# Reciprocals of the softmax sums broadcast as two f16 halves, with new instruction lists, in a four-batch transformer layer

## The reference

```
x = x + attn(layernorm(x)) ; x = x + ffn(layernorm(x))
attn: qkv = x @ Wqkv ; 16 heads of 32 ; a = softmax(mask(q k^T / sqrt(32))) ; (a @ v) @ Wo
ffn:  g = silu(x @ w1q^T) * (x @ w3q^T) ; g @ w2q^T      (w1, w3: 1365 x 512, w2: 512 x 1365)
ternary: s = mean|w| ; q = clip(round(w / s), -1, 1) * s
```

## Time and profile before

| | |
|---|---|
| three timed runs | 578.77, 579.03, 580.35 us (median 579.03) |
| the profiled execution | 580.78 us, of which the profile's span is 579.0 |
| TensorE busy | 508.0 us |
| VectorE, GpSimd, ScalarE busy | 411.8, 368.4, 330.2 us |
| mean granted TensorE clock | 0.941 of 2.4 GHz |

### The profile page before, as it was taken

One profiled execution on the slowest core, in us unless ns is written; L12 is line 12 of the kernel. 1 busy time (PEld: TensorE's weight loads), 2 busy tenths in 40 slices (PEclk: granted clock), 3 DMA queues, 4 the chain that ended last, 5 costly groups with the idle time before them and its releaser, 6 DMA issues.

```text
span 579.0 us, 11497 instructions
## 1 busy us (share of the span) xinstructions
PE 508.0 (88%) x4092; PEld 237.9 (41%) x4092; DVE 411.8 (71%) x1026; ACT 330.2 (57%) x833; POOL 368.4 (64%) x460
## 2 busy tenths in 40 slices
PE   2669754857999999999999999999999998839997
PEld 2224322333445444544444444454444454314443
DVE  6599787697899877966888879578878771523421
ACT  4769866777756875645467875363666752012320
POOL 3077689777968976776667887556668782312320
PEclk9689955878999999999999999999999999869999
DMA  8939978999889756387596565675783548030001
GB/s 312 316 30 278 193 170 160 252 200 211 153 141 162 145 124 131 56 158 194 108 167 143 90 131 97 141 180 114 101 173 75 109 87 208 9 63 1 0 37 72
DMA packets 224205, 79.52 MB, mean 137 GB/s; under 512 B 213226, under 2 KB 213226, under 8 KB 224148
## 3 DMA queue, kind: packets, MB, share of 16 engines
q1 hardware_dynamic: 224148, 78.79, 65.0%
HBM read 20.97 MB, written 4.19 MB: 43 GB/s over the span
## 4 chain that ended last, share of the span: by engine, by line
PE 69%; POOL 9%; DMA 8%; SPq 5%; DVE 4%; issue 2%; ACT 2%; DVEq 0%; ACTq 0%
PE work L1120 46%; PE work L1280 13%; DMA early<-early 4%; PE work L1239 4%; PE score_bank L1197 4%; POOL early L654 4%; PE work L1210 2%; DMA rows<-in_L_attn_x 2%; POOL late L687 2%; POOL early L687 1%; SPq L517 1%; DVE early L986 1%; DMA w_ternary<-early 1%; POOL rows L669 1%; DMA late<-rows 1%
## 5 line engine op out<-in xcount | busy, mean ns | idle before, releaser
L654 POOL TENSOR_TENSOR early<-early 128x512 f16<-128x512 f32 (+1 forms) x192 | 193.7, 1021 | 40.4 <-DVE early L986 26.5
L762 ACT ACTIVATE early<-early,exp_bias 128x512 f32<-128x512 f32 (+3 forms) x256 | 140.8, 551 | 76.7 <-POOL exp_bias L661 76.5
L1120 PE MATMUL work<-late,w_ternary 128*128 128x512 f16 (+1 forms) x704 | 158.9, 384 | 10.3 <-DMA late<-rows 10.3
L974 DVE CUSTOM_DVE_ANT_0 early<-score_bank,mask,scalars 128x512 f32<-128x512 f32 (+3 forms) x256 | 131.7, 543 | 32.7 <-POOL early L654 20.4
L986 DVE CAST early<-early 128x512 f16<-128x512 f32 (+1 forms) x148 | 99.5, 690 | 18.1 <-ACT early L762 14.7
L1120 PEld LDWEIGHTS work<-late,w_ternary 128*128 128x128 f16 (+1 forms) x704 | 69.2, 101 | 93.9 <-issue 17.9
L1120 PE MATMUL work<-xt,wqkv_hi 128*128 128x512 f16 x256 | 80.7, 398 | 2.9 <-DVE wqkv_lo L936 2.0
L1280 PE MATMUL work<-w_ternary,late 128*128 128x512 f16 (+1 forms) x352 | 77.7, 379 | 0.0
L679 POOL TENSOR_TENSOR late<-late 128x512 f16<-128x512 f32 (+1 forms) x44 | 51.3, 1168 | 40.1 <-ACT late L799 39.4
L792 ACT ACTIVATE late<-work,scalars 128x512 f32<-128x512 f32 (+1 forms) x44 | 30.0, 682 | 53.0 <-DVE late L1027 36.1
L1120 PE MATMUL work<-xt,wqkv_lo 128*128 128x512 f16 x128 | 51.0, 398 | 0.0
(11 more groups left out here) (103 smaller groups left out, 702.4 us busy)
## 6 DMA issues: line engine op xcount, KB each, us to landing
rows<-in_L_attn_x SPq DMA_DIRECT2D x16, 256.0 KB, 3.0
x_res<-in_L_attn_x SPq DMA_DIRECT2D x12, 256.0 KB, 3.2
out_y<-x_res SPq DMA_DIRECT2D x12, 256.0 KB, 2.8
late<-in_L_ffn_w SPq DMA_DIRECT2D x4, 682.5 KB, 5.5
early<-in_L_ffn_w SPq DMA_DIRECT2D x3, 768.0 KB, 12.8
late<-in_L_ffn_w SPq DMA_DIRECT2D x3, 768.0 KB, 6.7
late<-in_L_attn_Wqkv SPq DMA_DIRECT2D x4, 512.0 KB, 7.2
late<-in_L_attn_Wqkv SPq DMA_DIRECT2D x1, 1024.0 KB, 9.8
```

The costliest lines, as they stand in the source:

```text
L654: pool.tensor_tensor(split_view(s, p, 1, h), raw_view(s, p, h), split_view(s, p, 0, h), ALU.subtract).then_inc(low_done, 1)
L762: last = act.activation(piece, piece, ACT.Exp, bias=bias, accum_out=sums[:, s % 2, at:at + 1])
L974: last = dve.tensor_tensor_reduce(raws[n % RAWS][:, off:off + cols], score_bank[h][:, off:off + cols], mask[:, S - cols:S], scalar(exp_sca ...
L1120: last = pe.matmul(bank, lhs, rhs, start=(n == 0), stop=(n == len(terms) - 1))
```

## The change

The reciprocals are scaled by 2^24 and split in two f16 halves. The broadcast then takes two f16 products per head and row tile in place of one f32 product, accumulated in the same bank, and the copy out of the bank divides by 2^24. All five lists are replaced by new ones. SyncE's waits ahead of the transposes of x name the last readers per bank.

```diff
@@ constants and tiles
+INVERSE_UNIT = 2.0 ** 24
+        ident_half = sb("ident_half", [P, P], F16)
+        inverse_hi = sb("inverse_hi", [P, 2, ST * HG], F16)
+        inverse_lo = sb("inverse_lo", [P, 2, ST * HG], F16)
@@ SyncE, turn_rows
-                    for used in [(m, GROUPS * b - 1) for m in "qk"] + [("v", b - 1, j) for j in range(ST)]:
-                        full(sp, used)
+                    readers = [(m, GROUPS * (b - 1) + g) for m in "qk" for g in range(GROUPS)]
+                    readers += [("v", b - 1, j) for j in range(ST)]
+                    for n_bank in range(NW):
+                        full(sp, max((r for r in readers if bank_of(r) == n_bank), key=turn_of))
@@ GpSimd, constants
+                pool.wait_ge(ident_made, 1)
+                pool.tensor_copy(ident_half[:], ident[:]).then_inc(ident_turned, 1)
@@ ScalarE, inverse_copy
-                act.activation(o_sb[:], work[bank_of(step)][:], ACT.Copy).then_inc(work_free[bank_of(step)], 1)
+                act.activation(o_sb[:], work[bank_of(step)][:], ACT.Copy, scale=1 / INVERSE_UNIT).then_inc(work_free[bank_of(step)], 1)
@@ VectorE, invert
-                dve.reciprocal(inverse[:, s % 2, :], sums[:, s % 2, :]).then_inc(inverted, 1)
+                dve.reciprocal(inverse[:, s % 2, :], sums[:, s % 2, :]).then_inc(reversed_sums, 1)
+                dve.wait_ge(reversed_sums, s + 1)
+                dve.tensor_scalar(inverse_hi[:, s % 2, :], inverse[:, s % 2, :], INVERSE_UNIT, None,
+                                  ALU.mult).then_inc(inverse_hi_done, 1)
+                dve.wait_ge(inverse_hi_done, s + 1)
+                dve.scalar_tensor_tensor(inverse_lo[:, s % 2, :], inverse[:, s % 2, :], INVERSE_UNIT, inverse_hi[:, s % 2, :],
+                                         ALU.mult, ALU.subtract).then_inc(inverted, 1)
@@ TensorE, inverse_rows
+                if s == 0:
+                    pe.wait_ge(ident_turned, 1)
                 for u in range(ST):
-                    for h in range(HG):
-                        of_head = inverse[:, s % 2, u * HG + h:u * HG + h + 1].to_broadcast([P, HD])
-                        last = pe.matmul(work[bank][HD * h:HD * (h + 1), u * P:(u + 1) * P], of_head, ident[:],
-                                         start=True, stop=True, skip_group_check=True)
+                    for n, inv in enumerate((inverse_hi, inverse_lo)):
+                        for h in range(HG):
+                            of_head = inv[:, s % 2, u * HG + h:u * HG + h + 1].to_broadcast([P, HD])
+                            last = pe.matmul(work[bank][HD * h:HD * (h + 1), u * P:(u + 1) * P], of_head, ident_half[:],
+                                             start=(n == 0), stop=(n == 1), skip_group_check=True)
```

Of the lists, the parts that are spoken of below (the rest is laid out in the same manner, with steps moved by a few places):

```diff
@@ sp, the head
-        x_load:1,1 res_load:0,2 res_load:0,1 x_load:1,0 weight_turn:w1,0 res_load:0,0 weight_turn:w1,1
-        weight_load:w3,0 weight_turn:w1,2 weight_load:w3,1-2 probs_turn:0,0 weight_load:w3,3 probs_turn:0,1 xt:1,0-1
+        x_load:1,0-1 weight_load:w3,0-2 weight_turn:w1,1 weight_turn:w1,0 weight_load:w3,3 weight_turn:w1,2
+        probs_turn:0,0-2 res_load:0,3 xt:1,0-1 x_load:1,2 weight_load:w2,0 probs_turn:1,0 x_load:1,3 probs_turn:1,1
@@ dve, the head
-        split:1 stats_x:1,0 split:2-3 weight_mean:w1 split:8 q:0 split:4 k:0 wo_max max:0,0,0 split:5 max:0,0,1
-        split:6 q:1 max:0,0,2 high:0,0,0 max:0,0,3 split:7 high:0,0,1 q:2 max:0,1,0 high:0,0,2 max:0,1,1 high:0,0,3
+        top_turn:v split:1-2 stats_x:1,0 split:3 weight_mean:w1 split:8 q:0 k:0 split:4 stats_x:1,1 max:0,0,0
+        split:5-6 max:0,0,1 split:7 max:0,0,2 pad:w3 max:0,0,3 high:0,0,0 wo_max high:0,0,1-2 top_turn:wo
@@ pe, batch 0 to its gates
-        values:3 v:1,0-1 project:0,0 scores:4,2 project:0,1 v:1,2 scores:5,0 project:0,2-3 v:1,3 k:7 q:7 inverse:4
-        scores:5,1 values:4 gate:0,0
+        values:3 v:1,0-2 scores:4,2 project:0,0-2 scores:5,0 project:0,3 v:1,3 k:7 scores:5,1 inverse:4 q:7
+        values:4 gate:0,0
@@ pe, slots 10 and 11
-        scores:10,2 gate:1,8 lin:1,7-8 gate:1,9 lin:1,9 gate:1,10 scores:11,0 q:12 lin:1,10 k:12 scores:11,1
-        inverse:10 q:13 values:10 down:1,0 scores:11,2 down:1,1-2 scores:12,0 down:1,3 scores:12,1 inverse:11 k:13
-        values:11
+        scores:10,2 lin:1,7 gate:1,8-9 lin:1,8 scores:11,0 lin:1,9 gate:1,10 inverse:10 lin:1,10 scores:11,1 q:12
+        values:10 k:12-13 scores:11,2 down:1,0 scores:12,0 down:1,1 inverse:11 scores:12,1 q:14 values:11
@@ pe, the end of slot 15
-        lin:2,10 values:14 down:2,0 scores:15,2 down:2,1-2 inverse:15 down:2,3 values:15 project:3,0-3 gate:3,0-1
+        scores:15,2 down:2,0-1 inverse:15 down:2,2 values:15 down:2,3 project:3,0-3 gate:3,0-1 lin:3,0-1 gate:3,2-3
```

More of the change, by code:

```diff
@@ L86 @@
[L86 to L90, removed]
@@ L94 @@
+        down:3,3
     """,
     "pool": """
[L96 to L99 removed]
@@ new lines @@
+        high:7,0,3 max:7,1,1 q:9 max:7,1,2-3 gate:0,10 values:6 high:7,1,0 k:9 high:7,1,1 max:7,2,0 lin:0,10
+        high:7,1,2 max:7,2,1 high:7,1,3 max:7,2,2-3 stats_x:3,1 q:10 max:8,0,0-2 down:0,0 max:8,0,3 high:8,0,1 k:10
+        high:8,0,0 inverse:7 high:8,0,2 down:0,1 max:8,1,0 high:8,0,3 down:0,2 max:8,1,1 values:7 max:8,1,2-3
+        high:8,1,0-1 down:0,3 project:1,0 stats_y:1,0 high:8,1,2 norm_y:1,0 project:1,1 max:8,2,0 high:8,1,3
+        max:8,2,1-3 stats_y:1,1 project:1,2 v:2,0 stats_y:1,2 norm_y:1,1 v:2,1 project:1,3 max:9,0,0 stats_y:1,3
@@ L221 @@
+        max:15,2,2-3 values:14 inverse:15 down:2,1 down:2,0 down:2,2 values:15 project:3,0 down:2,3 stats_y:3,0
+        project:3,1 stats_y:3,1 norm_y:3,0-1 project:3,2 stats_y:3,2 project:3,3 stats_y:3,3 norm_y:3,2-3 gate:3,0
+        lin:3,0 gate:3,1 lin:3,1 gate:3,2 lin:3,2 gate:3,3 lin:3,3 gate:3,4 lin:3,4 gate:3,5 lin:3,5 gate:3,6
+        lin:3,6 gate:3,7 lin:3,7 gate:3,8 lin:3,8 gate:3,9 lin:3,9 gate:3,10 lin:3,10 down:3,0-3
     """,
     "pe": """
-        xt:0,0 xt:0,2 xt:0,1 xt:0,3 top_turn:qk top_turn:v q:0 weight_mean:w1 k:0 q:1 scores:0,0 q:2 top_turn:wo
@@ L239 @@
[L239 to L242 removed]
+        xt:0,1 xt:0,0 xt:0,2-3 top_turn:qk top_turn:v q:0 weight_mean:w1 k:0-1 scores:0,0 q:1 scores:0,1 top_turn:wo
+        v:0,0-1 scores:0,2 k:2 v:0,2 q:3 weight_mean:w3 scores:1,0 v:0,3 q:2 scores:1,1 inverse:0 k:3 values:0
@@ new lines @@
+        gate:0,9 lin:0,9 inverse:6 q:9 scores:7,1 gate:0,10 k:9 values:6 lin:0,10 scores:7,2 q:10 k:10 down:0,0
+        scores:8,0 down:0,1 scores:8,1 down:0,2 inverse:7 values:7 down:0,3 project:1,0 scores:8,2 project:1,1 v:2,0
+        project:1,2 v:2,1 project:1,3 scores:9,0 k:11 q:11 v:2,2 scores:9,1 v:2,3 inverse:8 gate:1,0 lin:1,0
+        gate:1,1 values:8 lin:1,1 scores:9,2 gate:1,2 lin:1,2 gate:1,3 lin:1,3 scores:10,0 gate:1,4 lin:1,4 gate:1,5
+        lin:1,5 scores:10,1 inverse:9 gate:1,6 values:9 lin:1,6 gate:1,7 scores:10,2 lin:1,7 gate:1,8-9 lin:1,8
@@ new lines @@
+        scores:11,0 lin:1,9 gate:1,10 inverse:10 lin:1,10 scores:11,1 q:12 values:10 k:12-13 scores:11,2 down:1,0
+        scores:12,0 down:1,1 inverse:11 scores:12,1 q:14 values:11 q:13 down:1,2 scores:12,2 project:2,0 v:3,0
+        project:2,1 scores:13,0 down:1,3 project:2,2 v:3,1 scores:13,1 project:2,3 inverse:12 v:3,2 k:15 v:3,3 k:14
+        values:12 scores:13,2 gate:2,0 lin:2,0 gate:2,1 lin:2,1 scores:14,0 gate:2,2 lin:2,2 gate:2,3 lin:2,3
+        scores:14,1 q:15 gate:2,4 inverse:13 values:13 lin:2,4 scores:14,2 gate:2,5 lin:2,5 gate:2,6 lin:2,6
@@ L243 @@
+        scores:15,0 gate:2,7 lin:2,7 gate:2,8 lin:2,8 scores:15,1 inverse:14 gate:2,9-10 lin:2,9 values:14 lin:2,10
+        scores:15,2 down:2,0-1 inverse:15 down:2,2 values:15 down:2,3 project:3,0-3 gate:3,0-1 lin:3,0-1 gate:3,2-3
+        lin:3,2-3 gate:3,4 lin:3,4 gate:3,5-6 lin:3,5-6 gate:3,7 lin:3,7 gate:3,8-9 lin:3,8-9 gate:3,10 lin:3,10
+        down:3,0-3
     """,
```

277 lines of the change are left out of this document (135 added, 142 removed).

## The result

The changed kernel takes 582.77 us (median of 8 runs, 579.74 to 585.4), the kernel before beside it 580.01 (8 runs). The ratio is 1.0057, 95% interval 1.003 to 1.0083: it is slower by 3.3 us, where 10 us less were forecast. So single marks of the two profiles can't be subtracted as they stand.

What follows compares the result with a forecast made beforehand. The prediction took TensorE's work to bound 160 to 480 us, and transfers and hand-overs the head. Its terms, -7.9 + 0.5 - 4.6 + 2 and 0 for the head, sum to -10.0: 579.0 to 569.0 us, range 564 to 576.5.

Steps and rivals of the forecast that it cites:

- The new step has eight such fours: 0.44 us: TensorE's inverse steps: f16 products take 0.44 us instead of 1.01 at full clock; -7.9 us in all.
- rival (a): Inverse steps: the f16 step is no shorter, as TensorE goes by instructions; 576.9 us, chance 0.05.
- One microsecond of products less is one microsecond less: From 160 to 480 us: TensorE's work is the bound, so shortened products shorten the kernel equally.
- I take 0.45 us a slot ... which covers it: VectorE's two added steps: 0.45 us a slot, covered by a 0.7 us gap in the full stretch; +0.5 us.
- Net 4.86 - 0.2 = 4.6 us saved: Last batch's lists: one down step moves behind values 15, filling TensorE's wait; -4.6 us.
- The mark of 505.9: Sign in the tail: the gates of the last batch start at about 505.9 us, before at 515.87.
- Rival (b): Last batch: the tail gives nothing, values 15 or the normalisation come later; 573.6 us, chance 0.13.
- I take +2: New lists in the full stretch: fewer products ahead of values and gates may open waits; +2 us, bounds 0 and 9.
- Values 10 and 11: Sign in the full stretch: new waits of several microseconds at these steps would show the forecast wrong.
- I take 0: New lists in the head, w3 loads ahead of w1 transposes on SyncE: 0 us, bounds -3 and +11.6.
- if the first gate of batch 0 came more than 3 us from 180.1: Sign at batch 0's first gates: a shift of more than 3 us would show the forecast wrong.
- Rival (d): Head: w3 loads block SyncE's queue and delay the w1 transposes by 11.6 us; 580.6 us, chance 0.06.

Runs made afterwards that it cites:

- e6: e1 without VectorE's two added steps: one reciprocal with f16 result used for both products, no scaling or low half; 576.23 us, ratio 0.9941.
- e1: The change of code on the five old lists of the kernel before; 579.08 us, ratio 1.0001.
- e5: The kernel before plus VectorE's two added steps, f32 products kept and nothing reading the halves; 584.47 us, ratio 1.0078.
- e13: e1 with the two added steps replaced by two more reciprocals, without scaling and low part; 576.75 us, ratio 0.9958.
- e9: The changed products with old lists up to the first gates of batch 0, new lists behind; 576.63 us, ratio 0.9951.
- e2: The old f32 products and single reciprocal on the new lists; 582.56 us, ratio 1.0065.
- e15: The kernel before, f32 products and one reciprocal, on e9's lists; 576.63 us, ratio 0.9962.
- e8: The changed products with new lists up to the first gates of batch 0, old lists behind; 584.47 us, ratio 1.0087.
- e12: The changed kernel with the first two w1 transposes ahead of the w3 loads in SyncE's list, the third behind one load; 591.17 us, ratio 1.0213.
- e16: The changed kernel with batch 0's steps from v to gates in old order on TensorE, VectorE, ScalarE, GpSimd; SyncE's list new; 584.12 us, ratio 1.008.
- e18: e16 with w2's last two transposes moved ahead of the second half of slot 4's probability transposes on SyncE; 578.64 us, ratio 1.0006.
- e10: e1 with both added steps reading one strided tensor, so neither has a second operand; 579.28 us, ratio 1.0001.
- e3: e1 with only the end of the lists new, down 2,3 behind values 15; 579.10 us, ratio 0.9993.

## Why the prediction was wrong, point by point

The forecast was a sum of five terms. Three failed: the products were worth less than half, VectorE's two steps cost 3 to 4 us more than was put down, and the head, put at nothing, cost most of all. The two terms for the lists behind the first gates came out right in their sum.

- **"The new step has eight such fours: 0.44 us", -7.9.** Right in kind: rival (a) is out, since the fours keep their pace of 0.055 us. But the sum took 0.055 us from the last four to the next step too, where it is 0.16. The step takes 0.56 us on the chain, so it saves 0.45, and the twelve of the full stretch save 5.4. Measured alone (e6) it is 3.4. "One microsecond of products less is one microsecond less" failed too: TensorE's waits grow as its work shrinks. In e6 it is busy for 316.3 of the 320 us, 1.8 less than before, and waits 2.9 us for the low halves of v where it waited 1.3. That covers most of the 2.0 us between 5.4 and 3.4.
- **"I take 0.45 us a slot ... which covers it", +0.5.** Measured 3.5 to 4.5 (e1 against e6, e5). Both bounds, 154 and 245 ns, came from forms that stay short. The view of before had the counter-example, which I didn't look for. VectorE's timeline has the same kind of step on 128x512 at 1.39 and at 0.55 us (lines below). A cover of 0.7 us does not hold 0.92, which is only the mean. Of the price, about 1 us is the work and the rest the standing still (e13). The waits that name inverse_lo are only 1.9 us between 160 and 480 us, in e1 and in e5; where the rest of the price is paid was not traced.
- **"Net 4.86 - 0.2 = 4.6 us saved", -4.6.** Right in kind, and for the changed kernel not far off: 4.0 us from the shared point to the last gates, 0.45 of it the shorter inverse step 15. On equal code (e9 against e1) it is 2.5. "It starts one down step earlier" holds: scores 15,2 come 3.6 us behind the shared point instead of 8.5. From there to the projection it takes 23.1 us instead of 20.6, since a down step stands where the wait of 2.85 stood, and values 15 wait 0.66 us for the last transpose. The stretch from the projection to the last gates then takes 21.0 us instead of 22.7: the half clock behind the wait is gone (0.61 in the windows of before at 493 to 497). But it comes in some executions only. With the old tail four of eight profiles have 22.5 to 22.7 us there and four have 21.0 to 21.1, e1 among them, with the same wait of 2.85 us; with the new tail all eleven have 21.0 to 21.1. So the 1.8 us of the term that stood for the half clock are to be had about half of the time. The mark of 505.9 failed by what was lost ahead of the tail. Rival (b) is out.
- **"I take +2", full stretch.** Measured by the profiles +0.4 (f16 products, e9 against e1) and +1.2 to +2.2 (f32 products, e2 and e15 against before). Values 10 and 11, where I expected waits, have none; the two new ones there are others, 0.93 us at inverse 10 for an emptied bank and 1.34 at q 12 for the transposed x. The sum with the tail is -2.9 (e9 against e1), forecast -2.6.
- **"I take 0", head.** Measured +4.9 (e8 against e1). The place I costed, w3 ahead of w1, did no harm: values 0 starts at 74.6, before at 76.0, and turning the order back costs 9 us (e12). Most of the loss lies where I had not looked, between values 3 and the first gates of batch 0: 38.0 us against 33.9. My own sign for it was "if the first gate of batch 0 came more than 3 us from 180.1". It came at 183.9. e16 to e18 show two causes that hide each other, late rows and late w2 transposes ahead of them in SyncE's queue; mending both gives back 3.0 of the 4.9 us. The rest is not explained.

The rows of before that the second point speaks of, VectorE's timeline; the first step starts 0.05 us behind a GpSimd instruction of 1.16 us (166.46):

```profile
166.51 1.39 DVE L882 TENSOR_SCALAR rows<-x_res,y_mean_var,y_rstd 128x512 f32<-128x512 f32 x1
...
172.55 0.55 DVE L882 TENSOR_SCALAR rows<-x_res,y_mean_var,y_rstd 128x512 f32<-128x512 f32 x1
```

Adding up: -3.4 (products) + 3.5 (steps) + 4.9 (head) - 2.9 (rest, tail within) = +2.1, measured +3.3 (1.7 to 4.8). Against the forecast of -10.0 the misses are 4.5, 3.0, 4.9 and -0.3.

Rival (d), the slower one, had the right sign and the wrong place. The chance of 0.07 for slower was far too low: each list had been replaced as a whole, and I gave a term of zero to what I couldn't read off.

Left open: some 2 us of the head; and why the changed kernel's runs spread over 5.7 us, the kernel before's over 3.0. The profiles only say where to look. Among the kernels with the old head the first gates come anywhere from 177.7 to 181.6, while the stretch from the shared point to the last gates is 47.2 to 47.8 us in ten of the eleven kernels with the new tail (48.6 in e16).

## What to carry to other kernels

Price a small added step by the longest duration of its kind beside a busy neighbour, not by the shortest; and ask for least, median and most, since means of 0.43 and 0.49 us hid steps of 0.17 and of 1.17. An edit that leaves in the trace what it was to take away (e10) tells little: look at the duration that it was to change before reading the time. Count a stretch from the last point at which both lists have done the same steps: by the bare mark of the last gates the tail seemed to give nothing, and it gave 4 us. When a list is laid anew, compare the moment at which each stage can begin on every queue, above all the last transfers of one stage that stand ahead of the first of the next, and test the list in cut pieces: here two parts were worth -2.9 and +4.9.

## What the runs showed of the hardware

VectorE's two added forms stand still behind GpSimd's passes over 256 or 512 columns. Undisturbed they take 0.174 us, beside such a pass up to 1.17, and then end 0.02 to 0.04 us behind it (175.88 + 1.15 against 175.85 + 1.15). The reciprocal of the same shape stayed at 0.24 to 0.25 in all 16 slots, beside the same passes too (slot 12 above), and so did the 48 reciprocals of e13. The Trainium skill states such a rule in "SBUF — State Buffer", section "Who interferes with whom": one pair of ports is shared by VectorE and GpSimd and locked for a whole instruction; a VectorE instruction meets GpSimd there when it has two SBUF inputs and GpSimd reads SBUF, or when it is a copy, cast or tensor_scalar in a two-port mode. The trace agrees for the step with two inputs (0.174 to 1.166 us). e10's one-operand step is a tensor_scalar, which the rule names as well, and it was held up to 1.135 us; which mode it ran in no view here shows. That the reciprocal stays outside is what the rows show. The rule would have warned of the VectorE term. The price here is the rest of GpSimd's instruction, up to 1 us.

Thirty-two f16 products of 128 columns, in fours side by side, take 0.56 us on the chain, 17.5 ns each, and the fours start 0.055 us apart, 14 ns for each product. The rule of about 25 ns between starts in the Trainium skill, "TensorE: Matmul & The Clock Gate", section "Wait — 56ns, not 53.3ns?", which the prediction weighs, does not hold for them.

A wait of TensorE is paid twice where its clock falls behind it: 2.45 us of wait in e3, then 5 us at a granted clock of 0.51. It does not always fall: behind the wait of 2.85 us ahead of the last projection the windows have 0.61 for the next 4 us in the kernel before and 1.00 in e1. In the changed kernel, after the 3.84 us at slot 4, the windows have 0.61:

```profile
173.00:177.20 4.20, 0.36 (x21) 0.22 (x16) 3.44 (x9) 1.11 (x2) 4.04 (x7) 1.00 1.00 184
177.20:181.60 4.40, 4.40 (x43) 1.85 (x44) 4.38 (x12) 1.82 (x4) 2.82 (x3) 0.61 0.57 106
```
